# First round of half B read by ScalarE into sums of its own, both halves' sums added to the scaled seeds by GpSimd, with new order tables

## What is computed

```
mask = adj > 0
h    = relu((x @ W1a)[:, :, None, :] + (x[:, :, None, :] - x[:, None, :, :]) @ W1b + b1)
hm   = einsum('bjkh,bjk->bjh', h, mask)          # H = 192, sum over the neighbours k of j
x    = layernorm(x + hm @ W2 + deg * b2)         # layer 0
x    = layernorm(x + gnn(x, adj))                # layer 1: two dense layers, A @ m, a GRU cell
```

## Time and profile before

| | |
|---|---|
| median of 3 runs | 804.84 us (804.28 to 804.87) |
| the profiled execution | 805.59 us, span 804.1 us |
| DVE busy | 762.4 us, 95% of the span |
| PE busy | 695.8 us, 87% |
| ACT busy | 640.9 us, 80% |
| POOL busy | 549.3 us, 68% |
| granted TensorE clock | 0.991 of full speed |
| DMA | 66.86 MB, 83 GB/s |

### The profile page before, as it was taken

The page is one execution under the profiler, slowest core; times in us unless marked ns, Lnnn a source line. Parts: engine busy times, 40 slices in busy tenths (PEclk is TensorE's granted clock), DMA queues, the critical chain, the costliest instruction groups (busy, mean ns, idle before and its releaser), DMA issues.

```text
span 804.1 us, 37406 instructions
## 1 busy us (share of the span) xinstructions
PE 695.8 (87%) x15984; PEld 568.7 (71%) x15984; DVE 762.4 (95%) x851; ACT 640.9 (80%) x1897; POOL 549.3 (68%) x625
## 2 busy tenths in 40 slices
PE   3768789889898989989899898989989898988885
PEld 2547677677787867768787777878677687867662
DVE  5799999999999999999999999999999999998983
ACT  5746676888888888888988888888988888887654
POOL 5534445677868677786867779696777969575772
PEclk9999999999999999999999999999999999999998
DMA  5533243233334323323323232433223243222000
GB/s 150 146 105 75 83 100 88 62 75 101 75 100 97 86 76 75 104 73 108 95 81 84 66 113 63 121 81 94 75 65 111 68 120 76 56 61 75 2 15 27
DMA packets 33316, 66.86 MB, mean 83 GB/s; under 512 B 5504, under 2 KB 6272, under 8 KB 33152
## 3 DMA queue, kind: packets, MB, share of 16 engines
q1 hardware_dynamic: 33152, 64.48, 30.3%
HBM read 22.52 MB, written 4.19 MB: 33 GB/s over the span
## 4 chain that ended last, share of the span: by engine, by line
issue 44%; PE 28%; DVE 21%; ACT 3%; DMA 2%; POOL 1%; SPq 0%; DVEq 0%; POOLq 0%
PE PS L649 20%; DVE AC L1196 11%; DVE AC L1217 7%; PE PS L903 3%; PE PS L968 2%; PE PS L723 2%; PE PS L886 1%; DMA VA<-VN 1%; DVE WM L1165 1%; ACT VN L1565 1%; DMA bs<-in_rows 1%; POOL MT L1780 0%; DVE AC L1212 0%; DVE DM L1175 0%; ACT YO L1484 0%
## 5 line engine op out<-in xcount | busy, mean ns | idle before, releaser
L1217 DVE SCALAR_TENSOR_TENSOR AC<-PS,AC 128x1152 f32<-128x1152 f32 (+4 forms) x288 | 333.2, 1157 | 11.6 <-PE PS L649 10.7
L1196 DVE SCALAR_TENSOR_TENSOR AC<-PS,AC 128x1152 f32<-128x1152 f32 (+4 forms) x256 | 291.0, 1137 | 1.6 <-PE PS L903 1.3
L649 PE MATMUL PS<-DM,VA 128*64 128x192 fp8e5 (+1 forms) x2048 | 126.4, 244 | 41.4 <-DVE AC L1196 29.5
L649 PEld LDWEIGHTS PS<-DM,VA 128*64 128x64 f16 x2048 | 81.3, 110 | 77.8 <-DVE AC L1196 49.6
L649 PE MATMUL PS<-DM,VB 128*64 128x192 fp8e5 (+1 forms) x2048 | 123.9, 240 | 0.7 <-DVE AC L1212 0.2
L903 PE MATMUL PS<-DM,VB 128*64 128x192 fp8e5 (+1 forms) x1024 | 85.9, 245 | 23.7 <-DVE AC L1217 19.2
L1175 DVE TENSOR_SCALAR DM<-CW 128x1536 uint16<-128x1536 uint16 (+1 forms) x132 | 96.2, 750 | 1.0 <-DMA CW<-WM 1.0
L649 PEld LDWEIGHTS PS<-DM,VB 128*64 128x64 f16 x2048 | 89.5, 110 | 2.6 <-DVE AC L1217 1.5
L1812 POOL TENSOR_TENSOR XE<-XQ,XT 128x512 f16<-128x512 f32 x32 | 41.3, 1289 | 70.2 <-ACT XT L1552 70.2
L1838 POOL TENSOR_TENSOR AC<-AC,SD 128x512 f32<-128x512 f32 (+1 forms) x62 | 65.3, 1063 | 29.4 <-DVE DM L1175 29.4
L903 PEld LDWEIGHTS PS<-DM,VB 128*64 128x64 f16 x1024 | 45.6, 108 | 54.1 <-DVE AC L1217 26.9
(11 more groups left out here) (240 smaller groups left out, 2067.5 us busy)
## 6 DMA issues: line engine op xcount, KB each, us to landing
CW<-WM SPq DMA_DIRECT2D x128, 160.0 KB, 2.8
XQ<-in_xq SPq DMA_DIRECT2D x32, 256.0 KB, 2.7
VA<-VN SPq DMA_DIRECT2D x64, 128.0 KB, 2.3
VB<-VN SPq DMA_DIRECT2D x64, 128.0 KB, 2.3
AT<-in_adjt SPq DMA_DIRECT2D x15, 512.0 KB, 4.6
XN<-in_xn SPq DMA_DIRECT2D x16, 256.0 KB, 4.4
...
```

The lines of the kernel that those rows point to most:

```text
L649: last = e.matmul(o[k], lhs[:, k], rhs, **flags)
L1196: e.scalar_tensor_tensor(t, tiles(PS[:, b + p:b + 3, :])[:, :, cols], 0.0, t, ALU.max, ALU.add).then_inc(s["sx"], 1)
L1217: e.scalar_tensor_tensor(t, tiles(PS[:, r, :])[:, :, cols], 0.0, t, ALU.max, ALU.add).then_inc(s["sy"], 1)
```

## The change

1. `round_b` with n = 1 goes from DVE to ACT, as a relu that writes a sum of its own, `BB[q % 2]` (two buffers, new). It waits for `ad` and `sov` of the quad two before. DVE's rounds b2 to b9 add to `BB`. For the last quad ACT does b1 in three pieces.
2. `AC` is now only half A's sum and six tiles of 192 dense columns. POOL's `clear` goes.
3. `add_u` becomes `add_a` and `add_b`: POOL adds the middle 128 columns of `AC`, then those of `BB`, to `SD` (the last quad's `add_b` is DVE's), and `out0_a` and `out0_b` read `SD` in place of `AC`. `s_ov` reads its half-A columns from `AC` and its half-B columns from `BB`.
4. a1 on ACT waits for `aa` (both `add_a` of the quad three before) in place of `o0`; `seeds` on ACT waits for `o0` in place of `ad`.
5. `VN`, `VA` and `VB` lose their zero columns 192 to 255: the DMAs into `VA` and `VB` are a quarter smaller, and two memsets in `setup` go.
6. All order tables are new. `rank_t` and `surplus` on PE get the waits that `HEAD`'s new order needs.

```diff
 ORDER = (
-    ("s2b", "pp3", "bp", "", "pe", "trprbd", "", "t", "te", "tpb", "pr", "epeee", "d", "pe", "", "pc", "d", "", "e0r1"),
-    ("sp", "dp", "2b3b", "dt", "p", "bt", "t", "et", "pr", "dlendpn", "", "pdd", "dp", "dcn", "pddb", "p", "pd", "0pd1", "r"),
+    ("e2p3bs", "", "rpbbd", "", "t", "p", "e", "rrp", "bt", "ptt", "pee", "edbpe", "pp", "e", "pd", "b", "d", "0", "1er"),
+    ("bsb2", "", "3d", "pp", "btb", "p", "dd", "p", "tlpt", "etd", "bnbdrd", "dp", "depdn", "p", "p", "dp", "dpnr", "0", "1"),
 )
...
-        VN = [sb(f"VN{i}", [128, 2, 4, 256], F16) for i in range(2)]
+        VN = [sb(f"VN{i}", [128, 2, 4, H], F16) for i in range(2)]
...
-        AC = [sb(f"AC{i}", [128, 3, 512]) for i in range(3)]
+        AC = [sb(f"AC{i}", [128, 6, H]) for i in range(3)]
+        BB = [sb(f"BB{i}", [128, 6, H]) for i in range(2)]
...
             def parts_of_u(t):
                 for k in range(2):
                     if t > 1:
-                        do("add_u", t - 2, k)
+                        do("add_b", t - 2, k)
+                    yield
+                for k in range(2):
+                    if t:
+                        do("add_a", t - 1, k)
                     yield
...
             def out0_a(q, b, gates):
-                    both(o, ac[:, i % 2, 256 * (i // 2) + 64:256 * (i // 2) + 192], w2s[:, 0, :], start=False, stop=True,
+                    both(o, sd[:, 2 * (i % 2) + i // 2, :], w2s[:, 0, :], start=False, stop=True,
...
             def round_b(q, n):                       # vector_main
 
+                if n == 1:
+                    return
                 b = 3 * (q % 2)
-                if n == 1:
-                    ve.wait_ge(s["clr"], q + 1)
-                    ve.wait_ge(s["sx"], 9 * q + 9)
                 cols = back if n <= C1 else nat if n < C0 else ninth
-                dst = tiles(AC[q % 3][:])[:, :, cols]
+                dst = BB[q % 2][:, :, cols.start - 64:cols.stop - 64]
...
+            def round_b(q, n):                       # scalar_main
+
+                if n > 1:
+                    return
+                b, dst = 3 * (q % 2), BB[q % 2][:]
+                ac.wait_ge(s["ad"], 2 * (q - 1))
+                ac.wait_ge(s["sov"], q - 1)
...
+                ac.wait_ge(s["gy"], 9 * q + 1)
+                t, r = (dst[:, tile[2]], slice(b + 1, b + 2)) if q == NQ - 1 else (dst, slice(b, b + 3))
+                e.activation(t, tiles(PS[:, r, :])[:, :, back], ACT.Relu).then_inc(s["sy"], 1)
...
-            def clear(q):
-                po.wait_ge(s["o0"], q - 2)
-                e.memset(tiles(AC[q % 3][:])[:, :, 192:256], 0.0).then_inc(s["clr"], 1)
...
+            def add_a(q, k):
+                h = slice(4 * k, 4 + 2 * k)
+                u = SD[q % 3][:, h, :]
+                po.wait_ge(s["im"], 2 * q + k + 1)
+                po.wait_ge(s["sx"], 9 * q + 9)
+                e.tensor_tensor(u, u, AC[q % 3][:, h, nat], ALU.add).then_inc(s["aa"], 1)
...
+            def add_b(q, k):
                 if q < NQ - 1:
+                    po.wait_ge(s["aa"], 2 * q + k + 1)
                     po.wait_ge(s["sy"], 9 * q + 9)
+                    e.tensor_tensor(u, u, BB[q % 2][:, h, 0:128], ALU.add).then_inc(s["ad"], 1)
```

More of the change, by code:

```diff
@@ L255, in build @@
         CW = [sb(f"CW{i}", [128, 2, 1280], U16) for i in range(3)]
[L256 to L258 removed]
+        VN = [sb(f"VN{i}", [128, 2, 4, H], F16) for i in range(2)]
+        VA = [sb(f"VA{i}", [128, 4, H], F16) for i in range(2)]
+        VB = [sb(f"VB{i}", [128, 4, H], F16) for i in range(3)]
         XE = [sb(f"XE{i}", [128, 4, 256], F16) for i in range(4)]
@@ L291, in build @@
         MSf = MS[:].rearrange("p k n -> p (k n)")
+        ACD = [t[:].rearrange("p (a b) n -> p a (b n)", b=2) for t in AC]
         SYf = SY[:].rearrange("p b n -> p (b n)")
@@ L604, in main_order @@
             for k in range(2):
-                do("add_u", NQ - 1, k)
+                do("add_b", NQ - 1, k)
             link = {"t": tail(NQ - 1), "n": link["n"], "d": link["d"]}
@@ L863, in surplus @@
                 pe.wait_ge(s["nvc"], 2 * g + 2)
+                pe.wait_ge(s["dc"], 16)
                 for name, v in gates:
@@ L1335, in vector_main @@
                                 "dgen": dgen, "round_a": round_a, "round_b": round_b,
-                                "wide_w": wide_w, "fold": fold, "s_ov": s_ov, "add_u": add_u, "bias": bias, "flag": flag, "fsum": fsum,
+                                "wide_w": wide_w, "fold": fold, "s_ov": s_ov, "add_b": add_b, "bias": bias, "flag": flag, "fsum": fsum,
                                 **vector_layer1(e, ve, s)})
@@ L1644, in scalar_main @@
             follow(main_order, {"soon": soon, "rank_n": rank_n, "split_x": split_x, "off": off, "ov": ov, "rank_t": rank_t, "rank_ov": rank_ov,
-                                "x_split": x_split, "x_turn": x_turn, "v": v, "v_low": v_low, "surplus": surplus, "seeds": seeds, "round_a": round_a, "s_ov": s_ov, "out0_c": out0_c,
+                                "x_split": x_split, "x_turn": x_turn, "v": v, "v_low": v_low, "surplus": surplus, "seeds": seeds, "round_a": round_a, "round_b": round_b, "s_ov": s_ov, "out0_c": out0_c,
                                 "fold": fold, "split_x1": split_x1, "split_h": split_h,
@@ L1846, in soon @@
                 hints.append((e, e.mark_branch_hint_location()))
-            follow(main_order, {"soon": soon, "setup": setup, "parts": parts, "count": count, "x_split": x_split, "split_x": split_x, "mask": mask, "split_xg": split_xg, "split_ms": split_ms, "split_x1": split_x1, "split_h": split_h, "s_ov": s_ov, "clear": clear, "scale_u": scale_u, "add_u": add_u, "dgen": dgen, **gpsimd_layer1(e, po, s)})
+            follow(main_order, {"soon": soon, "setup": setup, "parts": parts, "count": count, "x_split": x_split, "split_x": split_x, "mask": mask, "split_xg": split_xg, "split_ms": split_ms, "split_x1": split_x1, "split_h": split_h, "s_ov": s_ov, "scale_u": scale_u, "add_a": add_a, "add_b": add_b, "dgen": dgen, **gpsimd_layer1(e, po, s)})
         def gpsimd_dense(e):
```

75 lines of the change are left out of this document (37 added, 38 removed), and 2 rows, old and new, of the table MAIN.

## The result

| | before | after |
|---|---|---|
| median of the runs | 804.7 us (804.28 to 804.87) | 811.06 us (810.24 to 811.95) |
| ratio to before | | 1.0075, 95% interval 1.0059 to 1.0091 |
| the profiled execution | 805.59 us, span 804.1 | 811.95 us, span 807.4 |
| a pair of iterations, median of 15 | 46.58 us | 46.27 us |

A forecast was written before the change was run, and what follows sets the result against it. DVE was taken as the bound, PE nearly late in the seams. Seams gain 1.58 us a pair, less 0.4, so 1.2; over 15.5 pairs 18.6 us: 787.0 profiled, median 786, likeliest 775 to 796, eight in ten 766 to 803.

The forecast's parts named there:

- The even seam: From b9 to b2 in even iterations: b2 comes 0.75 us earlier, the middle of 0.45 and 1.0.
- The odd seam: From b9 to b2 in odd iterations: b2 at +5.55 instead of +6.38, 0.83 us gained, ACT and PE last.
- What the rounds give back: Moved PE work and two more ACT reads cost 0.4 us a pair, 0.1 of it m2 between a8 and b9.
- a1 "was read by an idle ACT": a1 behind b1 in ACT's queue ends up to 1.1 us later, hidden as long as ACT is in time.
- The lock (D): Planes and POOL's additions block each other: 14 us less gain, 800 us; chance 0.13 together with B.
- B: PE and ACT take the gain back in interior rounds: 0 to 0.6 us a pair left, 796 to 804; 0.13 with D.
- The head: Start of the kernel: two memsets go and loads change places, between -1 and +1 us, taken as 0.
- The tail: Last quad: b1 in three pieces on ACT costs nothing.
- Outside the span: No term of its own; the gain was subtracted from the whole profiled execution of 805.6 us.
- C: Slower, ACT becomes the bound: its waits for PE stay, two reads are added, 805 to 839 us; chance 0.12.
- what the profile was to show: Pair about 45.4 us, b2 at +5.5 and +5.1, DVE near 722 us, idle before b2 released by PE.

The follow-up runs named there:

- e9: Changed kernel with e8's head, and scale1, rank_n, x_split and scale2 moved behind a1, planes ahead of POOL's additions: 837.71 us, ratio 1.0412.
- e11: Changed kernel with one of PE's three products of each hidden-state gate matmul left out: 807.81 us, pair 45.88 us.
- e2: Kernel before with only the new HEAD table and the waits it needs in rank_t and surplus: 812.32 us, ratio 1.0075.
- e8: Changed kernel with the old HEAD table, the second group's load moved right behind the weights: 808.27 us, ratio 1.0044.
- f3: As e8, with the three pieces of the last quad's b1 read back on DVE: 807.76 us.
- e6: Changed kernel's new code under all the old order tables, clear dropped, add_a behind add_b: 857.29 us, ratio 1.0650.
- e5: Changed kernel with b1 read by DVE again, tables, buffers and POOL's part as changed: 840.76 us, ratio 1.0447.
- f2: Changed kernel with b1 back on DVE for quads 0 to 15, on ACT for 16 to 31: 828.9 us, ratio 1.0294.

## Why the prediction was wrong

The forecast was 787.0 for the profiled execution, 811.95 came. The difference of 24.95 us by its steps:

- **The even seam, forecast 0.75, measured 0.13.** This is the step that failed most within the pair: the wait for ACT's read of the seeds, which the sum put at nothing. Two errors. First, "the new table also moves `rank_n` ... to behind a1; that is 0.33 us off PE's chain": it isn't. Behind a1 is still ahead of b2, and the end of the seam is b2; the step was moved along the same chain. Second, I wrote down that ACT has `scale1`, the read of `rank_n` and `x_split` ahead of the seeds, and then charged nothing for it. They put the seeds' read to +2.93 and b1's to +3.69, and PE's a1, which needs the seeds' banks and stands ahead of b2, waited 0.91 us. The sum followed b2 through b1's reader and left out PE's own queue: seeds read, a1, `rank_n`, `surplus`, b2. Where the read of `rank_n` is missing, in the last seam of this kind, b2 comes at +5.13, which is 0.70 earlier than before: the forecast's size, for a seam without the step that it overlooked. e9 shows the same from the other side.
- **The odd seam, forecast 0.83, measured 0.61.** The seeds and b1 were read sooner than by the old order (b1 done at +4.46, forecast +4.72). What came last was the pair of planes, 2.56 in place of 1.89 us, and PE, which now has `A @ m` (1.07 us) between a1 and b2, where the step said that layer work leaves. The direction was right, a quarter of its size lost.
- **What the rounds give back, forecast 0.4 a pair, measured 0.43.** Right in size, by luck in part, since most of the 0.4 was a guess between two bounds; not at b9, where I put it, but ahead of b6 of the odd iteration (0.43 us of wait), and PE's load is its cause there (e11).
- **a1 "was read by an idle ACT": a misreading.** Before the change ACT had been idle for only 2.4 us ahead of all 32 reads of a1 together. The conclusion, that a later a1 is hidden, held: in the kernel after DVE waits for nothing ahead of a2 in either seam.
- **The lock (D).** Planes cost 16 us more DVE time, where I allowed 7. The trace agrees with the Trainium skill ("SBUF — State Buffer", section "Who interferes with whom") in that the two engines hold each other up: 0.55 us for a plane alone, 1.03 to 1.32 in the groups beside POOL's operations. In the even seam this is hidden behind PE, in the odd one it is level with PE.
- **Together** the pair gave 0.31 and not 1.2: 18.6 - 4.65 = 13.95 us of the miss. B said "0 to 0.6 us a pair is left", and that is what the pair did, though the rounds gave back only 0.43 us, and the rest was never won in the seams.
- **The head, "taken as 0", between -1 and +1: +4.86.** The diff showed that the weights' loads stand ahead of the adjacency's, and the chain to the first planes begins with the adjacency. I priced the places of the loads and not the queue behind them: DVE's first mask moved from 3.43 to 8.71. e2 and e8 confirm it.
- **The tail, taken as "nothing": +1.71.** Not the three pieces on ACT (f3). b2 of the last quad isn't late: it comes 4.77 us after the last b9, before 7.27, for all that DVE waits 3.56 us for PE ahead of it. Its b3 is level with before (+10.42, +10.36). Then b3 to b4 takes 3.71 us, before 1.41: DVE has five sums of the weights (`ft`) and a plane between them, and in the kernel before it made these sums ahead of b1. Counted from the last b9, the quad's own round 9 comes 3.75 us later than before, and the rest of the tail gets back 2. From 779 to 782 the granted clock is half too (full there before), where DVE waits 0.20 and 0.43 us for PE. No run was made on `LAST` and `END`.
- **Outside the span: +3.06**, a part that the forecast carried over unchanged. Nothing in the profile of before pointed to it.
- **Iterations off the pattern: +1.4.**

13.95 + 4.86 + 1.71 + 3.06 + 1.4 = 25.0 us, within rounding. For the sign the pair alone doesn't decide: between the b9s the change does gain 3.3 us. Head, tail and what is outside the span, each held at zero, turned that into a loss; none of my rivals had such a part. The slower case that I named (C, ACT as the bound) was right as a mechanism for 1.9 of the 3.2 us that a pair loses under the old order (e6), and wrong for this change, whose tables avoid it. The move itself is worth 2.2 us a pair (e5, f2), but against a table that costs 1.9 a pair (48.46 - 46.58, b1 on DVE in both). I had set the move against the old table's seam and let the new one be free.

Of what the profile was to show: ACT 674.4 us (forecast 676), POOL 610.7 (604), b1's read directly behind the seeds: as said. Idle time before b2 released by PE: in the even seam only. DVE 741.4 in place of 722, mostly by the planes' 16; b2 at +5.77 and +5.70 in place of +5.5 and +5.1; window of a pair 46.26 in place of 45.4: not.

None of the versions with the move beats the kernel before. The nearest are e11, which leaves work out, f3 (807.76) and e8 (808.27); all three have the 3 us outside the span.
